# The last stage's attention sums: turned by two transposing transfers in place of TensorE, with GpSimd's coefficients in mid-turn

## The reference, cut to what matters

```python
h = einsum('bhid,oi,od->bho', x, weighted_sum, weight)       # stage 1: token mixing
h = concatenate([h, txt], axis=1)                            # 8 x 589 tokens of 256
h = h + attn(layernorm(h))                                   # stage 2: 16 heads over the batch of 8

# stage 3, for each token by itself: attention between its own 16 heads, then 8 experts
h1  = rmsnorm(layernorm(h), gamma1)
q   = (h1 @ Wq + bq).reshape(b, t, 16, 16)
k,v = split((((h1 @ Wdown + bdown) @ Wup) + bup).reshape(b, t, 16, 32), 2, axis=-1)
att = softmax(einsum('bthd,btgd->bthg', q, k) / 4)
out = einsum('bthg,btgd->bthd', att, v).reshape(b, t, 256)   # the normalised sums: fon
x   = layernorm(h) + (out @ Wo + bo)
h2  = rmsnorm(x, gamma2)
y   = x + sum over e of softmax(h2 @ Wg + bg)[e] * (h2 @ We[e])
return h + y
```

## Time and profile before

| what | us |
|---|---|
| time, median of 3 runs (775.63 to 776.11) | 775.76 |
| time of the profiled execution | 773.28 |
| its span, first to last instruction | 771.3 |
| TensorE busy in the span | 735.3 (95%) |
| VectorE busy | 666.3 (86%) |
| GpSimd busy | 404.4 (52%) |
| ScalarE busy | 373.6 (48%) |
| from turn 3's first matmul of stage 3 to turn 36's | 367.6 |

### The profile page before, as it was taken

One profiled execution on the slowest core, in us unless ns is written; L12 is line 12 of the kernel. 1 busy time (PEld: TensorE's weight loads), 2 busy tenths in 40 slices (PEclk: granted clock), 3 DMA queues, 4 the chain that ended last, 5 costly groups with the idle time before them and its releaser, 6 DMA issues.

```text
span 771.3 us, 48239 instructions
## 1 busy us (share of the span) xinstructions
PE 735.3 (95%) x20274; PEld 505.1 (65%) x20274; DVE 666.3 (86%) x1591; ACT 373.6 (48%) x985; POOL 404.4 (52%) x1094
## 2 busy tenths in 40 slices
PE   3999988999999999978899999999999999999998
PEld 2888865777776777756556666666666666666653
DVE  4789757899999999977678988898898889889986
ACT  4478634566666666634343444444444444443431
POOL 1151255565666667735455656566555655565421
PEclk9999998999999999998999999999999999999999
DMA  9987100000000000000101100110011001100100
GB/s 325 319 272 214 51 2 4 0 0 0 0 0 0 0 0 0 10 18 10 24 18 28 27 25 16 27 27 24 17 27 27 24 17 27 27 20 21 28 15 20
DMA packets 38365, 33.05 MB, mean 43 GB/s; under 512 B 24786, under 2 KB 33570, under 8 KB 38314
## 3 DMA queue, kind: packets, MB, share of 16 engines
q1 hardware_dynamic: 38314, 32.35, 14.0%
HBM read 22.64 MB, written 4.83 MB: 36 GB/s over the span
## 4 chain that ended last, share of the span: by engine, by line
PE 79%; DVE 3%; issue 3%; POOL 1%; ACT 0%; DVEq 0%; POOLq 0%
PE bank L191 17%; PE bank L193 15%; PE bank L192 15%; PE bank L967 6%; PE bank L956 6%; PE bank L274 5%; PE bank L284 5%; PE bank L975 2%; PE bank L200 1%; PE bank L994 1%; PE bank L306 1%; PE bank L1028 1%; PE bank L1046 1%; PE bank L1029 1%; PE bank L294 1%
## 5 line engine op out<-in xcount | busy, mean ns | idle before, releaser
L191 PE MATMUL bank<-we_h,h_t_h 128*128 128x512 f16 x296 | 113.4, 383 | 2.0 <-DVE acc L1275 0.9
L193 PE MATMUL bank<-we_h,h_t_l 128*128 128x512 f16 x296 | 112.9, 381 | 0.2 <-issue 0.2
L192 PE MATMUL bank<-we_l,h_t_h 128*128 128x512 f16 x296 | 112.7, 381 | 0.0
L1275 DVE SCALAR_TENSOR_TENSOR acc<-bank,gate,acc 128x256 f32<-128x256 f32 x222 | 100.5, 453 | 5.0 <-PE bank L193 4.5
L191 PE MATMUL bank<-tokw_h,x_t_h 128*128 128x256 f16 x256 | 71.0, 277 | 12.3 <-DVE x_t_l L689 12.2
L192 PE MATMUL bank<-tokw_l,x_t_h 128*128 128x256 f16 x256 | 71.0, 277 | 0.0
L193 PE MATMUL bank<-tokw_h,x_t_l 128*128 128x256 f16 x256 | 71.0, 277 | 0.0
L967 PEld LDWEIGHTS bank<-fpr_t,v 32*32 32x32 f32 x4736 | 47.8, 104 | 22.0 <-issue 21.5
L1164 ACT ACTIVATE junk<-x 128x256 f32<-128x256 f32 x37 | 15.4, 417 | 92.9 <-DVE x L1328 92.9
L967 PE MATMUL bank<-fpr_t,v 32*32 32x32 f32 x4736 | 52.8, 194 | 6.0 <-issue 6.0
L1284 DVE TENSOR_REDUCE smax<-bank 128x16 f32<-128x512 f32 x37 | 25.6, 692 | 38.0 <-PE bank L956 38.0
(11 more groups left out here) (223 smaller groups left out, 2211.3 us busy)
## 6 DMA issues: line engine op xcount, KB each, us to landing
xbuf<-in_x SPq DMA_DIRECT2D x32, 512.0 KB, 5.4
out<-res SPq DMA_DIRECT2D x36, 128.0 KB
we_s<-in_we SPq DMA_DIRECT2D x4, 512.0 KB, 6.7
inw<-in_in_w SPq DMA_DIRECT2D x1, 768.0 KB, 10.7
hn_t_h<-hn_r_h SPq DMA_TRANSPOSE x37, 2.3
hn_t_l<-hn_r_l SPq DMA_TRANSPOSE x37, 2.4
wrep<-in_w_rep SPq DMA_DIRECT2D x1, 512.0 KB, 5.5
h_all<-in_txt SPq DMA_DIRECT2D x1, 512.0 KB
```

What stands on the lines that cost most here:

```text
L191: nc.tensor.matmul(dst, a_h(c), b_h(c), start=start and c == 0, stop=False)
L192: nc.tensor.matmul(dst, a_h(c), b_l(c), start=False, stop=False)
L193: last = nc.tensor.matmul(dst, a_l(c), b_h(c), start=False, stop=stop and c == chunks - 1)
L1275: nc.vector.scalar_tensor_tensor(out=(res if e == E - 1 else acc)[:, :], in0=b_we[s % 2][:, k * D:(k + 1) * D], scalar=gate[p][:, e:e + 1] ...
```

## The change

It takes the turning of `fon` off TensorE. ScalarE writes the high half of `fon` as it lies, with tokens on the partitions (`halved`, at the end of its turn, semaphore `f_onh`), GpSimd the low half (at the end of its turn, `p_onl`), and SyncE sends both by transposing transfers into `fon_h` and `fon_l` (`on_in`, 16 a transfer). `projected` waits for 32 x i of `on_in`. `turned`, its eviction and VectorE's low half go. `turned_x2`, now the only user of `b_turn`, takes over the wait for stage 2's last use of that bank. GpSimd's coefficients move from the end of its turn to behind `lat_l`. SyncE's loop is written anew: result of tile i-3, `hn` of tile i+3, `fon` of tile i.

```diff
@@ buffers @@
+        on_r = halves("on_r", [P, D])
@@ TensorE @@
-            def turned(i):
-                if real(i, -1):
-                    pe.wait_ge(f_on, i)
-                    wait(pe, f_h2l, i - 1)
...
-                        last = nc.tensor.transpose(b_turn[:, c * P:(c + 1) * P],
-                                                   fon[:, :, :].rearrange("p h d -> p (h d)")[:, c * P:(c + 1) * P],
-                                                   ident[:, :])
-                    last.then_inc(f_onps, 1)
@@ projected @@
                 if real(i, -1):
-                    pe.wait_ge(f_onl, i)
+                    pe.wait_ge(on_in, 32 * i)
                     wait(pe, f_logit, i - 1)
@@ TensorE body and join @@
                 gated(i, p)
-                turned(i)
                 asked(i)
@@ ScalarE; halved(i) is called behind rows(i), turned(i) is no more @@
-            def turned(i):
-                if real(i, -1):
-                    act.wait_ge(f_onps, i)
-                    wait(act, f_wo, i - 1)
-                    nc.scalar.activation(fon_h[:, :, :], b_turn[:, 0:D], ACT.Copy).then_inc(f_onh, 1)
+            def halved(i):
+                if real(i, 0):
+                    act.wait_ge(f_on, i + 1)
+                    wait(act, on_in, 32 * i)
+                    nc.scalar.activation(on_r[0][:, :], fon[:, :, :], ACT.Copy).then_inc(f_onh, 1)
@@ VectorE @@
-                if real(i, -1):
-                    dve.wait_ge(f_onh, i)
-                    nc.vector.tensor_tensor(fon_l[:, :, :], b_turn[:, 0:D], fon_h[:, :, :], ALU.subtract).then_inc(f_onl, 1)
...
                     dve.wait_ge(f_rsum, i + 1)
-                    wait(dve, f_onps, i)
+                    wait(dve, p_onl, i)
@@ GpSimd, behind lat_l @@
+                if real(i, AHEAD) and real(i, 0):
+                    ffn_coefficients(pool, i + AHEAD)
@@ GpSimd, at the end @@
-                if real(i, AHEAD) and real(i, 0):
-                    ffn_coefficients(pool, i + AHEAD)
+                if real(i, 0):
+                    pool.wait_ge(f_onh, i + 1)
+                    nc.gpsimd.tensor_tensor(on_r[1][:, :], fon[:, :, :].rearrange("p h d -> p (h d)"), on_r[0][:, :],
+                                            ALU.subtract).then_inc(p_onl, 1)
@@ SyncE, the new loop @@
+                for i in range(-3, TILES + 3):
+                    if real(i, -3):
...
+                        sp.wait_ge(f_comb, (i - 2) * STEPS)
+                        sp.dma_start(out[at:at + rows, :], res[0:rows, :]).then_inc(out_done, 16)
+                    if real(i, 3):
+                        j = i + 3
+                        sp.wait_ge(f_hn, j + 1)
+                        wait(sp, f_down, j)
+                        sp.dma_start_transpose(hn_h[:, :, :], hn_r[j % 2][0][:, :]).then_inc(hn_in, 16)
+                        sp.wait_ge(p_hnl, j + 1)
+                        sp.dma_start_transpose(hn_l[:, :, :], hn_r[j % 2][1][:, :]).then_inc(hn_in, 16)
+                    if real(i, 0):
+                        sp.wait_ge(f_onh, i + 1)
+                        wait(sp, f_wo, i)
+                        sp.dma_start_transpose(fon_h[:, :, :], on_r[0][:, :]).then_inc(on_in, 16)
+                        sp.wait_ge(p_onl, i + 1)
+                        sp.dma_start_transpose(fon_l[:, :, :], on_r[1][:, :]).then_inc(on_in, 16)
```

More of the change, by code:

```diff
@@ L926, in build @@
         names = ("f_hn", "p_hnl", "hn_in", "f_q", "f_down", "f_lat", "f_qraw", "f_qpad", "f_kv", "f_kvt", "f_qt",
-                 "f_s", "f_max", "f_sub", "f_exp", "f_prt", "f_av", "f_of", "f_rsum", "f_on", "f_onps", "f_onh", "f_onl",
+                 "f_s", "f_max", "f_sub", "f_exp", "f_prt", "f_av", "f_of", "f_rsum", "f_on", "on_in", "f_onh", "p_onl",
                  "f_wo", "f_x2", "f_ss2", "f_logit", "f_h2ps", "f_h2h", "f_h2l", "f_gate", "f_gmax", "f_gexp", "f_grec",
@@ L930, in build @@
         (f_hn, p_hnl, hn_in, f_q, f_down, f_lat, f_qraw, f_qpad, f_kv, f_kvt, f_qt,
-         f_s, f_max, f_sub, f_exp, f_prt, f_av, f_of, f_rsum, f_on, f_onps, f_onh, f_onl,
+         f_s, f_max, f_sub, f_exp, f_prt, f_av, f_of, f_rsum, f_on, on_in, f_onh, p_onl,
          f_wo, f_x2, f_ss2, f_logit, f_h2ps, f_h2h, f_h2l, f_gate, f_gmax, f_gexp, f_grec,
@@ L984, in gated @@
                     rows_times(b_gate, *h2_t[p], lambda c: wg_h[:, c, :], lambda c: wg_l[:, c, :]).then_inc(f_gate, 1)
-            def turned(i):
-                if real(i, -1):
-                    pe.wait_ge(f_on, i)
-                    wait(pe, f_h2l, i - 1)
-                    if isinstance(i, int) and i == 1:
-                        pe.wait_ge(a_sub, TILES)
-                    for c in range(KC):
-                        last = nc.tensor.transpose(b_turn[:, c * P:(c + 1) * P],
-                                                   fon[:, :, :].rearrange("p h d -> p (h d)")[:, c * P:(c + 1) * P],
-                                                   ident[:, :])
-                    last.then_inc(f_onps, 1)
             def asked(i):
@@ L1044, in turned_x2 @@
                     pe.wait_ge(f_x2, i)
+                    if isinstance(i, int) and i == 1:
+                        pe.wait_ge(a_sub, TILES)
                     for c in range(KC):
@@ L1086, in join @@
                     scored(t)
-                    turned(t)
                     asked(t)
@@ L1209, in body @@
                 rows(i, p)
+                halved(i)
             def join(i):
@@ L1228, in join @@
                     rows(t, 0)
+                    halved(t)
                 elif t == 1:
-                    turned(t)
                     asked(t)
@@ L1462, in _ @@
             def _(sp):
[L1463 to L1471, removed]
+                for i in range(-3, TILES + 3):
+                    if real(i, -3):
+                        at = (i - 3) * P
                         rows = min(P, TOKENS - at)
-                        sp.wait_ge(f_comb, (i - 3) * STEPS)
+                        sp.wait_ge(f_comb, (i - 2) * STEPS)
                         sp.dma_start(out[at:at + rows, :], res[0:rows, :]).then_inc(out_done, 16)
+                    if real(i, 3):
[11 more added lines that the diff above has]
+                        sp.dma_start_transpose(fon_l[:, :, :], on_r[1][:, :]).then_inc(on_in, 16)
                 sp.wait_ge(out_done, TILES * 16)
```

1 line of the change is left out of this document (removed).

## The result

The changed kernel takes **984.68 us** (median of 4 runs, 982.67 to 988.12) against 775.69 us for the kernel before: 1.271 times as long, interval 1.268 to 1.275. That is 209 us more; 977 us had been forecast. The profiled execution's span is 982.6 us against 771.3, 211.3 more.

What follows compares the result with a forecast made beforehand. TensorE was taken to bound the kernel; 160 us (transfers) + 42 (clock) + 0.5 (ends) - 1 (turn 2's gap) = 201.5 on 773.28 us gave about 975, set at 977 us with the runs' median; range 927 to 1005.

Steps and rivals of the forecast that it cites:

- What bounds, and where the stall lies: Last stage: TensorE bounds; it would idle some 5 us a turn before projected, waiting for fon behind hn's pair.
- The chain's sum: SyncE's queue from down to fon's low half landed: projected 4.94 us late, less 0.25 removed, +4.7 us a turn, 160 us.
- The clock: TensorE's idle time brings one clock fall in each of 34 turns: 1.25 us a turn, 42 us.
- rival B: Each turn's clock fall lasts twice as long, 3.4 us a turn over 34 turns: 1049 us, chance 0.07.
- The first turns: Turns 1 and 2 pay 5.95 us each, less 1 for half of turn 2's 2.02 us gap: 10.9 us.
- The ends: Turns 35 to 37: +1.3 us for fon's low half in turn 37, less 0.25 three times: +0.5 us.
- GpSimd's move: GpSimd's coefficients behind lat_l: norm's steps up to 1.7 us later, qpad and lat_l up to 1.6 earlier; booked at nothing.
- A: The clock holds through TensorE's gaps, leaving only the transfers' delay: 935 us, chance 0.15.
- C: SyncE's fon transfers get out ahead and land before projected; 35 x 0.25 = 9 us gained: 767 us, chance 0.03.
- D: SyncE's 1.17 us holding is waiting, not issue cost; delay shrinks to 2.1 us a turn: 847 us, chance 0.04.

Runs made afterwards that it cites:

- swapped pairs: Changed kernel with SyncE's two pairs of a turn swapped, fon of tile i before hn of tile i+3: 763.73 us, 0.990 of the kernel before.
- two buffers: Changed kernel with two buffers for the turned hn, whose pair waits for the down of a turn before: 804.33 us, ratio 1.042.
- filled kernel: Changed kernel with 38 spare 256-column matmuls on TensorE ahead of the wait in projected, in the loop's turns: 937.27 us, ratio 1.214.
- plain transfers: Changed kernel with 28 spare matmuls in the stall and fon's two transfers sent plain, not turned: 899.62 us (one run).

## Why the prediction was right

**What bounds, and where the stall lies: right.** TensorE stands before `projected` and nowhere else for long. The four transfers start at `down`'s end; the two kernels that change only what `fon`'s pair stands behind (swapped pairs, two buffers) are 221 and 180 us shorter.

**The chain's sum: right.** Forecast from rows of the kernel before: issue 0.3 us after `down`'s last matmul begins, 1.21 + 1.28 + 1.21 of holding, 2.4 to land, together 4.94 us late. Measured: 0.30, then 1.21 + 1.34 + 1.23, and 2.39; `projected` came 6.47 us after that matmul where it had come 1.42 before, 5.05 late. Less the turning, 4.7 was forecast; the filled kernel's turn gives 4.66.

**The clock: right in kind, the term mis-sized.** I took 1.25 us a turn, inside the bounds of 0 and 1.7 for one stretch of 3.4 us a turn. It measured 1.70 in the mean, 0.45 more, 14 us over 32 turns; the range held it. Two things make it up. In the 20 turns with one stretch the term is 17.21 - 15.80 = 1.41: the fall was expected inside the wait, so that part of the stretch would be free, and it came at the wait's end, with at most 0.43 us free. That is 5 of the 14 us. The other 9 come from the 12 turns with a stretch twice as long, 17.98 - 15.80 = 2.18. The sum had no such turns; they stood in rival B alone, as every turn and at 3.4 us. In eight of these twelve the stretch did begin inside the wait, 1.9 to 2.8 us before its end, as the forecast had pictured it. That the mean equals the upper bound of 1.7 is chance: with 19 spare matmuls a stretch wholly on work cost 1.3 to 1.6. The Trainium skill's rule (TensorE: Matmul & The Clock Gate, "HAM oscillation"), by which each burst behind a wait for a DMA starts cold, agrees with this trace nearly to the letter: each of turns 1 to 34 has its low stretch, and in six the burst runs up to 0.33 us at 1.00 before it.

**The first turns: the saving underrated.** Turns 1 and 2 cost 8.3 us instead of 10.9. Turn 1 pays in full (6.2 us more than before), turn 2 only 2.5, with a wait of 4.96. Its gap of 2.02 us, put down to issue and counted at half, is gone from the changed kernel's trace. And behind that gap the kernel before already ran 3.3 us at 0.50, so the forecast charged turn 2 for a fall that it had paid for before. No run parts the two.

**The ends: about right.** Turn 37 waits 1.33 us for `fon`'s low half, 1.3 was worked out; the stretch from turn 35 on came out at -0.2 instead of +0.5.

**GpSimd's move: right here, too short in its reach.** Booked at nothing, it measured nothing in the changed kernel. The working looked only at what the move delays; it did not ask what the turn would be with `fon`'s low half on GpSimd and the coefficients left in place. With the stall gone, that is worth 22 us.

**The rivals.** A (the clock holds) is the filled kernel, and needs spare work. C (the transfers get out ahead) gave 767 us in the text; the swapped pairs, which get them out ahead, took 763.73 beside a kernel before of 772.72, 9.0 us gained as worked out. But the way to it that C names, an `hn` pair that waits for the `down` of a turn before, is the kernel with two buffers, and that took 804.33: C had left out that the `hn` pair would still hold the queue 2.5 us ahead of `fon`'s. (B's 1049 should be 1051 by the sum used for the others; nothing hangs on it.) D (the holding is a waiting for the transfers) fell with the plain transfers. The Trainium skill (DMA: Bandwidth & Descriptors, "Issuing engines are not separate DMA queues") calls the time on the sequencer to initiate a DMA usually small relative to the DMA itself. The traces here do not bear that out: 0.54 us against a median of 1.9 to land for a plain transfer, 1.2 against 2.4 for a transposing one.

**Luck in the total.** The span grew by 211.3 us where 201.5 had been added up: 14 too little for the clock, against 1.3 too much for the transfers, 2.6 for the first turns and 0.7 for the ends. The misses partly cancel.

## What to carry to other kernels

A queue that only issues transfers is still a list in order: before a transfer is put into it, ask what the entries ahead of it wait for and when that comes. Here the right place was ahead of one other pair of transfers, and worth some 220 us. Work moved off the bounding engine gains what it cost there (0.25 us a turn here) only when its new path ends before its reader begins; and once it does, the helper that took it over (GpSimd here) may be the next to be late, so its other work has to be moved along. A stall on TensorE is to be priced with the clock: 4.7 us of waiting cost 6.4 a turn.

## What the runs showed of the hardware

- A transposing transfer of 128x256 or 128x512 float16 from SBUF to SBUF holds SyncE 1.17 to 1.25 us, at either size, but for a few (3 of the 148 in the changed kernel took 1.7 to 2.5); a plain one of 128x256 float16 0.46 to 0.60. Two halves sent as one save a whole holding: the turn is 14.6 us against 15.8.
- Idle time of TensorE in each turn of some 16 us, and the granted clock: 0.65 us, 1.00, no fall in 28 turns; 1.7 us, 0.95 to 0.97 over stretches of 100 us, a fall in some turns; 2.7 us, 0.90, a fall each turn; 4.8 us, 0.87, a fall each turn, twice as long in 12 of 32. Between 2.7 and 4.8 us of idle time the kernel's time hardly changed (982.18 and 984.68 us).
- Spare matmuls in a wait of 4.8 us a turn kept the clock at 1.00 and made the changed kernel 47 us faster (984.68 to 937.27).
